# A mixture-of-convolutions layer on one NeuronCore: four neighbouring pixels on a partition, and the 3x3 convolution as 15 products instead of 35

## What is computed

```python
xc = conv2d(group_norm(x, 32 groups), conv1_w, conv1_b)   # 1x1: 768 -> 16 channels
h = mean(xc, (rows, columns)) @ H_w.T + H_b               # one logit for each of 4 experts
g = softmax(h where h is among its two largest, else -inf)
for i in range(4):                                        # expert i
    up = resize(xc, 2**i times larger, bilinear)
    up = conv2d(up, convl_w, convl_b)                     # 3x3, 16 -> 16 channels
    experts[i] = resize(up, back to 64 x 64, bilinear)
out = sum(experts[i] * g[i])
return x + conv2d(out, conv2_w, conv2_b)                  # 1x1: 16 -> 768 channels
```

## Time and profile before

| | |
|---|---|
| median of three runs | 1451.96 us (1449.88 to 1457.01) |
| span of the profiled execution | 1451.0 us |
| TensorE matmul busy | 1189.7 us, 82% |
| VectorE busy | 1029.3 us, 71% |
| ScalarE busy | 661.9 us, 46% |
| GpSimd busy | 313.9 us, 22% |
| moved by DMA | 540.01 MB, mean 372 GB/s |

### The profile page before, as it was taken

How to read it: one execution, slowest core, us unless ns; L and a number is a source line. 1 busy time by engine, 2 the same in 40 slices (tenths; PEclk the granted TensorE clock), 3 DMA queues, 4 the chain that set the end, 5 groups by cost and what they waited for, 6 DMA issues and landing times.

```text
span 1451.0 us, 24055 instructions
## 1 busy us (share of the span) xinstructions
PE 1189.7 (82%) x8700; PEld 814.9 (56%) x8700; DVE 1029.3 (71%) x2747; ACT 661.9 (46%) x1549; POOL 313.9 (22%) x381
## 2 busy tenths in 40 slices
PE   0679999988987999789968899887787899779863
PEld 0466676656654777466546666555555665445531
DVE  6869988678469897764797884569766755636654
ACT  3578999553423797545225784411551352100110
POOL 1083003403041000340540001065004104344100
PEclk9989999999986999799978999978898898667865
DMA  9798897499999999999999998999999999999999
GB/s 344 256 359 318 301 370 288 176 392 319 399 366 416 409 389 349 378 395 387 392 412 411 390 377 288 388 396 402 416 390 344 399 411 414 417 416 410 401 416 388
DMA packets 188162, 540.01 MB, mean 372 GB/s; under 512 B 12810, under 2 KB 12810, under 8 KB 188044
## 3 DMA queue, kind: packets, MB, share of 16 engines
q1 hardware_dynamic: 118140, 336.75, 61.4%
q10 hardware_dynamic: 69904, 201.74, 34.9%
HBM read 337.12 MB, written 201.33 MB: 371 GB/s over the span
## 4 chain that ended last, share of the span: by engine, by line
PE 45%; DMA 23%; DVE 16%; ACT 5%; issue 5%; SPq 4%; POOL 1%; ACTq 0%; DVEq 0%; POOLq 0%
PE ring_ps L680 16%; DMA x_sb<-in_x 12%; DMA out<-x_sb 10%; PE conv_ps L750 10%; DVE x_sb L1010 9%; PE img_ps L697 8%; PE ring_ps L781 8%; DVE stats L926 7%; SPq L521 3%; ACT xT L803 2%; PE ring_ps L710 1%; SPq L494 1%; PE ring_ps L769 1%; ACT unread_squares L831 1%; ACT unread_copy L833 1%
## 5 line engine op out<-in xcount | busy, mean ns | idle before, releaser
L1010 DVE TENSOR_TENSOR x_sb<-x_sb,ring_ps 128x768 f32<-128x768 f32 x512 | 462.1, 950 | 299.5 <-PE ring_ps L781 215.8
L926 DVE BATCH_NORM_STATS2 stats<-x_sb 128x6 f32<-128x192 f32 x1792 | 473.0, 344 | 36.7 <-DMA x_sb<-in_x 26.8
L803 ACT COPY xT<-ring_ps 128x1024 f32<-128x1024 f32 x384 | 377.0, 1012 | 194.1 <-PE ring_ps L680 130.7
L781 PE MATMUL ring_ps<-w,es 128*128 128x512 f32 (+1 forms) x1024 | 335.8, 447 | 126.0 <-DVE x_sb L1010 107.7
L680 PE MATMUL ring_ps<-ident,x_sb 128*128 128x128 f32 x3072 | 402.4, 284 | 25.2 <-DVE x_sb L1010 10.4
L680 PEld LDWEIGHTS ring_ps<-ident,x_sb 128*128 128x128 f32 x3072 | 351.5, 146 | 101.9 <-issue 56.0
L781 PEld LDWEIGHTS ring_ps<-w,es 128*128 128x128 f32 x1024 | 190.9, 232 | 250.1 <-DVE x_sb L1010 169.2
L643 POOL TENSOR_TENSOR band<-taps,masks 128x640 f32<-128x640 f32 (+1 forms) x112 | 132.9, 1203 | 515.7 <-PE conv_ps L750 511.9
L697 PE MATMUL img_ps<-xT,w 128*32 128x256 f32 x3072 | 216.2, 389 | 16.2 <-ACT xT L803 15.2
L750 PE MATMUL conv_ps<-xc,band 128*128 128x1 f32 (+8 forms) x1120 | 221.4, 346 | 0.7 <-POOL band L643 0.7
L750 PEld LDWEIGHTS conv_ps<-xc,band 128*128 128x128 f32 x1120 | 159.0, 198 | 69.9 <-issue 67.3
(11 more groups left out here) (94 smaller groups left out, 361.1 us busy)
## 6 DMA issues: line engine op xcount, KB each, us to landing
x_sb<-in_x SPq DMA_DIRECT2D x128, 1536.0 KB, 11.3
out<-x_sb ACTq DMA_DIRECT2D x256, 768.0 KB, 9.8
x_sb<-in_x SPq DMA_DIRECT2D x172, 768.0 KB, 9.3
w_rep<-in_L_conv_conv_w ACTq DMA_DIRECT2D x1, 384.0 KB
wl_raw<-in_L_conv_convl_w SPq DMA_DIRECT2D x8, 9.0 KB
gate_w<-in_L_conv_H_w SPq DMA_DIRECT2D x8, 0.2 KB
w_raw<-in_L_conv_conv_w SPq DMA_DIRECT2D x1, 48.0 KB
b_raw<-in_L_conv_conv_b SPq DMA_DIRECT2D x2, 3.0 KB
```

The costliest lines, as they stand in the source:

```text
L781: last = nc.tensor.matmul(flat_ps[:, buf, part], es4[:, q, (i % 4) * P:(i % 4 + 1) * P], w2[:, part], start=True, stop=True)
L803: nc.scalar.copy(xT[:, at % XT], ring_ps[:, TURN["T", a, n] % RING]).then_inc(xT_copied, 1)
L926: ins = nc.vector.bn_stats(stats[:, c, g, :], group)
L1010: nc.vector.tensor_tensor(x_sb[:, n, 2 * half + q % 2, :], x_sb[:, n, 2 * half + q % 2, :], flat_ps[:, TURN["E", b, t] % RING, 0:D], ALU.a ...
```

## The change

The pixels are laid out anew. A partition holds four neighbouring pixels, 4 x 768 float32 that are one run of 12 KB in HBM. A slot is a group of 16 image rows x every second group of four columns; half slots are runs of 6 KB. With this the 128 partitions of `xc` are the image's columns modulo eight x 16 channels, so an image row's neighbours lie in the free dimension and a column's neighbours lie across partitions. The convolution then has five parts, one for each row tap (MID, LEFT, RIGHT and the two border rows), and three products in a part: a block-tridiagonal matrix `tri` on `xc`; `wrap`, for columns whose neighbour is in the next group of eight, on `shifted`, a shifted copy of the image; and `edge`, for the border columns, on `borders`. GpSimd makes `shifted` and `borders` by four copies (`shift_image`), and builds each part's three matrices with seven instructions.

```diff
-    slots_of = "b (q p j bb) w c -> b p j (bb w) q c"
-    x_v = x.rearrange(slots_of, q=QN, p=2, j=4, bb=2)
+    slots_of = "b (g y) (v s q) c -> b s g (y v) (q c)"
+    x_v = x.rearrange(slots_of, g=4, y=HH // 4, v=NV, s=2)
...
-MAT_ORDER = [HERE, FROM_ABOVE, UP, FROM_BELOW, DOWN, TOP, BOTTOM]
-NM = len(MAT_ORDER)
+ROW_TAPS = [MID, LEFT, RIGHT, LEFT_EDGE, RIGHT_EDGE]
+NM = len(ROW_TAPS)
...
+            def shift_image(b):
+
+                at = XC_PLACE[b]
+                link(nc.gpsimd.tensor_copy(borders[0:32, :, 0:1], xc_v[0:32, at, :, 0:1]))
+                link(nc.gpsimd.tensor_copy(shifted[0:32, :, 0:NV - 1], xc_v[0:32, at, :, 1:NV]))
+                link(nc.gpsimd.tensor_copy(shifted[96:P, :, 1:NV], xc_v[96:P, at, :, 0:NV - 1]))
+                nc.gpsimd.tensor_copy(borders[96:P, :, 1:2], xc_v[96:P, at, :, NV - 1:NV]).then_inc(image_shifted, 1)
+                pool.wait_ge(image_shifted, BI[b] + 1)
...
             for bi, b in enumerate(B_ORDER):
-                pool.wait_ge(gates_ready, b // 4 + 1)
+                pool.wait_ge(xc_copied, AI[b] + 1)
                 if bi:
                     pool.wait_ge(band_ready, NM * bi)
-                    pool.wait_ge(band_used, NM * bi - BANDS + 1)
-                weigh_taps(b, bi)
-                for part, m in enumerate(MAT_ORDER):
+                    pool.wait_ge(band_used, NM * bi)
+                shift_image(b)
+                pool.wait_ge(gates_ready, b // 4 + 1)
+                weigh_taps(b)
+                for part, tap in enumerate(ROW_TAPS):
...
+                    for ax in (LEFT, MID, RIGHT):
+                        ins = nc.gpsimd.tensor_tensor(
+                            products[:, ax], taps[:, tap, ax].unsqueeze(1).broadcast_to([P, NH, R]),
+                            masks[:, TAP_MASK[ax]].unsqueeze(2).broadcast_to([P, NH, R]), ALU.mult)
+                    link(ins)
+                    link(nc.gpsimd.tensor_tensor(tri[:, at], products[:, LEFT], products[:, MID], ALU.add))
...
+                    nc.gpsimd.tensor_tensor(tri[:, at], tri[:, at], products[:, RIGHT], ALU.add).then_inc(band_ready, 1)
...
+                    pe.wait_ge(image_shifted, BI[b] + 1)
...
-                for ax in (MID, LEFT, RIGHT, LEFT_EDGE, RIGHT_EDGE):
...
+                nc.tensor.matmul(conv_v[:, rows_out], tri[:, n % BANDS].rearrange(flat),
+                                 xc_v[:, XC_PLACE[b], rows_in], start=(part == 0), stop=False)
+                nc.tensor.matmul(conv_v[:, rows_out], wrap[:, n % BANDS].rearrange(flat),
+                                 shifted[:, rows_in], start=False, stop=False)
+                last = nc.tensor.matmul(conv_v[:, rows_out, 0:NV:NV - 1], edge[:, n % BANDS].rearrange(flat),
+                                        borders[:, rows_in], start=False, stop=(part == NM - 1))
```

```diff
-E2.31 C1.3-6 X1.0-1
+E2.31 C1.3-4 X1.0-1
```

More of the change, by code:

```diff
@@ L22 @@
 QN = 4
+NV = WW // NH
 SPS = 8
@@ L203 @@
 NT = 5
[L205 to L208, removed]
-MAT_ORDER = [HERE, FROM_ABOVE, UP, FROM_BELOW, DOWN, TOP, BOTTOM]
-NM = len(MAT_ORDER)
+SAME, NEXT, BEFORE = range(3)
+TAP_MASK = [NEXT, SAME, BEFORE]
+ROW_TAPS = [MID, LEFT, RIGHT, LEFT_EDGE, RIGHT_EDGE]
+NM = len(ROW_TAPS)
 def resize_taps():
@@ L237, in resize_taps, with row_ranges @@
     return coef
[L240 to L252, removed]
+def row_ranges(tap):
+    return {LEFT: (slice(1, HH), slice(0, HH - 1)), MID: (slice(0, HH), slice(0, HH)),
+            RIGHT: (slice(0, HH - 1), slice(1, HH)), LEFT_EDGE: (slice(0, 1), slice(0, 1)),
+            RIGHT_EDGE: (slice(HH - 1, HH), slice(HH - 1, HH))}[tap]
 def step_chunk(n):
@@ L394, in program @@
         es4 = sb("es4", [P, QN, PIX], F32R)
-        band = sb("band", [P, BANDS, NT, NH, R])
+        tri = sb("tri", [P, BANDS, NH, R])
+        wrap = sb("wrap", [P, BANDS, NH, R])
+        edge = sb("edge", [P, BANDS, NH, R])
+        of_taps = sb("of_taps", [P, NT * NT * R])
+        shifted = sb("shifted", [P, HH, NV])
+        borders = sb("borders", [P, HH, 2])
         ring_ps = ctx.enter_context(nc.psum_tensor("ring_ps", [P, RING, QN, 2 * P], F32))
@@ new lines, in _ @@
+                shift_image(b)
+                pool.wait_ge(gates_ready, b // 4 + 1)
+                weigh_taps(b)
+                products = of_taps[:, 0:3 * NH * R].rearrange("p (x h r) -> p x h r", x=3, h=NH)
+                for part, tap in enumerate(ROW_TAPS):
+                    n = NM * bi + part
+                    at = n % BANDS
+                    if part:
+                        pool.wait_ge(band_ready, n)
+                        if n >= BANDS:
+                            pool.wait_ge(band_used, n - BANDS + 1)
+                    for ax in (LEFT, MID, RIGHT):
[4 more added lines that the diff above has]
+                    link(nc.gpsimd.tensor_tensor(tri[:, at], products[:, LEFT], products[:, MID], ALU.add))
+                    nc.gpsimd.tensor_tensor(wrap[:, at, 0:NH:NH - 1], taps[:, tap, LEFT:RIGHT + 1:2],
+                                            ends[:, 0:2].unsqueeze(2).broadcast_to([P, 2, R]), ALU.mult)
+                    nc.gpsimd.tensor_tensor(edge[:, at, 0:NH:NH - 1], taps[:, tap, LEFT_EDGE:RIGHT_EDGE + 1],
+                                            ends[:, 1:3].unsqueeze(2).broadcast_to([P, 2, R]), ALU.mult)
+                    nc.gpsimd.tensor_tensor(tri[:, at], tri[:, at], products[:, RIGHT], ALU.add).then_inc(band_ready, 1)
@@ L739, in conv @@
             def conv(b, part):
-                m = MAT_ORDER[part]
                 n = BI[b] * NM + part
                 if part == 0:
+                    pe.wait_ge(image_shifted, BI[b] + 1)
                     pe.wait_ge(xc_copied, AI[b] + 1)
@@ L746, in conv @@
                 pe.wait_ge(band_ready, n + 1)
-                for ax in (MID, LEFT, RIGHT, LEFT_EDGE, RIGHT_EDGE):
-                    blk_out, blk_in = blk_ranges(m)
-                    col_out, col_in = column_ranges(ax)
-                    last = nc.tensor.matmul(
-                        conv_v[:, blk_out, col_out], band[:, n % BANDS, ax].rearrange("p h r -> p (h r)"),
-                        xc_v[:, XC_PLACE[b], blk_in, col_in],
-                        start=(part == 0 and ax == MID), stop=(part == NM - 1 and ax == RIGHT_EDGE))
+                rows_out, rows_in = row_ranges(ROW_TAPS[part])
+                flat = "p h r -> p (h r)"
+                nc.tensor.matmul(conv_v[:, rows_out], tri[:, n % BANDS].rearrange(flat),
[4 more added lines that the diff above has]
+                                        borders[:, rows_in], start=False, stop=(part == NM - 1))
                 last.then_inc(band_used, 1)
```

89 lines of the change are left out of this document (47 added, 42 removed).

## The result

The changed kernel takes **1489.66 us** (median of four runs, 1487.06 to 1491.35), beside 1451.93 us for the kernel before on the same chip (median of four). The ratio is 1.0246 with a 95% interval of 1.0219 to 1.0273: 38 us slower. The profiled execution has a span of 1489.2 us.

A forecast was written before the change was run, and what follows sets the result against it. Bound in stages: DMA in thirteen of 40 slices, elsewhere DMA is starved, with TensorE's convolution setting the end at sample 3. 1451.0 + 50 + 8 - 10 - 17 - 8 - 5 = 1469, forecast 1470 us, range 1453 to 1488.

The forecast's parts named there:

- what the pauses cost: TensorE waiting for GpSimd at six samples' convolutions: 54 us left, taken as +50, with bounds of 27 and 54.
- TensorE's saving: Convolution work on TensorE falls from 12.9 to 7.3 us a sample, 90 us in 16 samples, worth nothing where DMA bounds.
- GpSimd's lateness: GpSimd's work behind each image's copy: 12.7 us to the first part, then 3.0 us a part; TensorE stands at six samples.
- 4 us of cover: Taken off the stalls' 54 us for sample 7, which stands among tiles at full DMA.
- 10 us of slack: Delays partly made good where TensorE waits for others between the six places: -10, between 0 and 20 us.
- The clock's +8: TensorE's clock is low after six pauses of over 10 us: up to 1.6 us each, +8, or 0.
- DMA's -17: Longer runs gain 2.5% on thirteen slices at 401 GB/s or more (12 us), half that on twelve slices below (5 us).
- The start's -8: With 128 runs a load instead of 512, SyncE gets ahead and VectorE's whole wait of 7.74 us goes: -8.
- Elsewhere, -5: Samples 4, 8 and 10, partly in starved slices, keep some of TensorE's saving: -5 of 3 x 5.6 us.
- DMA carries it: Rival, 25 slices at 387 GB/s or more: longer runs give 4% (44 us), stalls cost 27, time 1416 us; chance 0.20.
- The stalls are swallowed: Rival: transfers and VectorE catch up behind each pause, only 30 us of the 50 remain, 1450 us; chance 0.14.
- The runs don't help: Rival: longer runs gain nothing, so the DMA, start and slack terms go, 1505 us; chance 0.13.

The follow-up runs named there:

- e7: The changed kernel with SBUF padding between a partition's pixels, so that every DMA run stays at 3 KB; 1509.24 us, ratio 1.0374.
- e1: The changed kernel with GpSimd's summing of a sample's taps moved ahead of the wait for its image; 1449.85 us, ratio 0.9979.
- e2: The changed kernel with taps and the first three parts' matrices built ahead of the wait for the image, the four copies behind it; 1429.04 us, ratio 0.9853.
- e3: The kernel before, with GpSimd's taps put behind the waits for the sample's image and all of the last convolution; 1504.98 us, ratio 1.0367.
- e6: The changed kernel with taps and three parts' matrices ahead of the image wait, and padding that keeps DMA runs at 3 KB; 1447.93 us, ratio 0.9952.
- e5: The changed kernel with taps and three parts' matrices ahead of the image wait, and late weights issued after the 16th load, not the 13th; 1425.83 us, ratio 0.9811.

## Why the prediction came out as it did

The forecast was 1470 us, slower by 18, for the right reason; it is slower by 38, just above the forecast's own range of 1453 to 1488. Of the 20 us between, 12 lie in what the pauses cost (43 forecast, 55 measured) and some 8 in what the longer runs bring, the start included (25 forecast, 17 measured, 1509.24 - 1489.66 less 2.4 for the two runs of the kernel before). Step by step:

- **TensorE's saving was sized well.** A part at full clock took 1.91 us with 504 columns and 0.59 at the border (sample 3 of the changed kernel), where 1.95 and 0.70 were worked out.
- **GpSimd's lateness was sized well.** Forecast latency 12.7 us, measured 12.3; parts every 3.0 us, measured 2.65. The six places are the six named, with 11.4, 10.1, 12.5, 12.5, 11.4 and 11.4 us forecast and 11.2, 10.4, 12.0, 12.0, 10.9 and 10.9 measured.
- **What the pauses cost was set too low; this step failed.** The terms that make up the change without its longer runs were +50, +8, -10 and -5, so +43; `e7` is that kernel, 1509.24 - 1454.36 = 55 us over its own runs of before. The credits failed: 4 us of cover and 10 us of slack. Without them the same terms give +57 (with the clock's 8, which is not shown). The cover was for sample 7, whose pause of 12.0 us left a step of 12.0 in the table of lags (31.1 to 43.1, between 128 and 160 additions). The argument for slack, that TensorE works only 36.67 of 39 us, does not hold: `e1`, `e2` and `e3` say so three times (46 us of pauses for 40, the table of lags, 47.9 for 52.8). The small gaps seem to be waits within the same chain, which move along with it; that is argued, not shown. Queued transfers do run on through a pause (394 GB/s at sample 2), but they ran out behind it (270 GB/s from 336.7 to 340, 80 from there to 348), and nothing of that reached the end.
- **The clock's +8** is not shown as a term of its own. The granted clock was indeed low behind each pause (0.52 for 4.1 us at sample 3, which is near 1.2 GHz). But the last matrix of that sample was ready at 276.37 and the convolution ended at 277.7, so that a full clock could have brought it at most 0.7 us sooner: at sample 3 GpSimd was late anyway, the case that the prediction put at 0. The other five places were not looked at. How the 55 us split between what the pauses leave, the clock and TensorE's shorter convolution was not separated.
- **DMA's -17 had about the right size.** The runs bring 14 to 20 us, but with what they do at the start, for which the forecast had another 8. The rise of the ceiling was a little less than taken (416 to 424 GB/s is 1.9%, not 2.5%). Here the rule of the Trainium skill (DMA: Bandwidth & Descriptors, Why small descriptors are slow), by which joining is only worth it at 256 bytes and below, would have had 0; `e6` and `e7` show 1.0 to 1.3% of the time instead. That sentence is about packing consecutive descriptors into one packet. Here the descriptors themselves grow, which is near it but not the same, so the runs show that it does not carry over, not that it is false. The two packet rows that stood against it (a fixed 7 ns in 121.6) pointed the right way: 4 x 121 ns became 460.
- **The start's -8 failed.** Its step was that with 128 runs a load "SyncE gets ahead, and the weights fall under the loads". SyncE got ahead with the loads, and lost it again on the weights, 4.4 us each instead of 2.0. And `e5`, which does remove the wait, shows that 7 us at the start leave 0.2 at the 32nd addition. The whole wait was the wrong price: in the changed kernel it did not go, and in `e5`, where it goes, it is worth 3 us by the medians and 6 by the ratios, which the intervals do not tell from nothing.
- **Elsewhere, -5:** `e6` has the new products without the pauses at the six places and without the longer runs, and stands 5.7 us under its runs of before. That the sum agrees is in part luck: by the count of additions `e6` is ahead of the kernel before by 5.5 us at 64, when samples 3 and 2 are through, by 7.7 at 160 and by 3.0 at the end, so samples 4, 8 and 10 did not bring it alone. TensorE's busy time is 66 us lower in `e6` (1189.7 to 1123.2; the forecast had 90) for a gain of 6: most of what it saved was not on the path that sets the end.

The rivals: **DMA carries it** needed the runs to outweigh 35 us; they bring under 20. Its 44 us also stood on 1100 us, while the 25 slices that it names are 25 x 36.3 = 908 us, and 4% of that is 36. **The stalls are swallowed** falls with the table of lags. **The runs don't help** did not happen, but `e7` builds it: 1509 us, where 1505 was worked out.

## What to carry to other kernels

When a change gives a helper engine one new input, look at what else stands behind that wait on its queue: here four copies needed the image, and 10 us of work that did not need it went along, which cost some 60 us; moved back ahead of the wait, the same change is 1.5% faster than the kernel before (1.9% with the weights issued later, which is not clear of the first). Look at DMA behind a pause, not ahead of it: pauses of 10 to 12 us, behind which DMA fell to 270 GB/s or less, cost nearly their full length, with no credit for slack, though DMA had moved 392 to 422 GB/s ahead of most of them. The one of 5.9 us through which and behind which DMA went on at 424 GB/s cost nothing. Runs of 3 KB were within 1.3% of runs of 12 KB here, so longer ones are worth having only if their layout costs no wait.

## What was not expected of the hardware

The time that SyncE needs to issue the same transfer of 9 KB depends on what fills its queue: 2.0 us each behind loads of 3 KB runs (before, and 16.20 / 8 in `e6`), 4.4 us behind loads of 12 KB runs, 0.66 us three loads later, and 5.3 us from ScalarE while SyncE's loads of 12 KB runs were under way. So fewer and longer runs in the large transfers can make the small ones behind them slower. Why is only argued: a queue seems to hold a fixed number of runs and to take a new one when an old one is done, which lasts nearly four times as long when it is four times as big (460 ns for 121). The issue time rose only 2.2 times, so that can't be the whole account.
